# A new order of issue for four engines in a six-layer attention and feed-forward kernel

## The reference

```
for i in range(6):
    x = attn_layer(shift_tokens(x), Wqkv[i], q_scale[i], k_scale[i], Wo[i]) + x
    x = ffn_layer(shift_tokens(x), ln_g[i], ln_b[i], W1[i], b1[i], W2[i], b2[i]) + x
# attn_layer: q, k, v = split(x @ Wqkv); q, k = l2norm(q) * qs, l2norm(k) * ks
#             q, k rotated (cos and sin tables); softmax(8 q k^T, each window of 32 with the one before) @ v; @ Wo
# ffn_layer:  a, gate = split(layernorm(x) @ W1 + b1); a * gelu(gate) @ W2 + b2   (341 inner columns)
```

## Time and profile before

| | |
|---|---|
| median of 3 runs | 3438.64 us (3437.9 to 3438.7) |
| the profiled execution | 3438.64 us, its span 3436.9 us |
| granted TensorE clock, mean | 0.997 |
| PE busy | 3384.2 us (98%) |
| PE weight loads | 2885.9 us (84%) |
| ACT busy | 3077.6 us (90%) |
| DVE busy | 2999.8 us (87%) |
| POOL busy | 2471.8 us (72%) |

### The profile page before, as it was taken

How to read it: one execution, slowest core, us unless ns; L and a number is a source line. 1 busy time by engine, 2 the same in 40 slices (tenths; PEclk the granted TensorE clock), 3 DMA queues, 4 the chain that set the end, 5 groups by cost and what they waited for, 6 DMA issues and landing times. The chain is left out here.

```text
span 3436.9 us, 178950 instructions
## 1 busy us (share of the span) xinstructions
PE 3384.2 (98%) x70388; PEld 2885.9 (84%) x70388; DVE 2999.8 (87%) x7016; ACT 3077.6 (90%) x10549; POOL 2471.8 (72%) x2057
## 2 busy tenths in 40 slices
PE   8999989999999999999999999999999999999998
PEld 5666678888888888888888888888888888888887
DVE  8999989888988888888888988889888888888987
ACT  8999978899999999989999999999999999998886
POOL 0121178787878878788787887878878788787784
PEclk9999999999999999999999999999999999999999
DMA  2000012111221111121111121112211111111111
GB/s 106 8 5 20 5 41 60 49 44 43 54 61 49 46 43 48 55 56 54 41 48 50 55 58 44 49 40 56 59 48 49 41 47 54 50 44 47 53 44 45
DMA packets 177482, 160.67 MB, mean 47 GB/s; under 512 B 113933, under 2 KB 124813, under 8 KB 176397
## 3 DMA queue, kind: packets, MB, share of 16 engines
q1 hardware_dynamic: 176653, 149.22, 15.4%
HBM read 25.71 MB, written 4.19 MB: 9 GB/s over the span
## 5 line engine op out<-in xcount | busy, mean ns | idle before, releaser
L1547 POOL TENSOR_TENSOR a_rn<-a_ssqc,a_minus_half 128x16 f32<-128x16 f32 x384 | 1114.2, 2901 | 477.8 <-DVE a_ssqc L1758 477.2
L1431 ACT ACTIVATE late<-bank,a_negmax 128x64 f32<-128x64 f32 x3072 | 926.6, 326 | 21.3 <-DVE a_negmax L1709 19.4
L1565 POOL TENSOR_TENSOR a_r<-a_u,a_rn 128x512 f32<-128x512 f32 x768 | 806.1, 1050 | 55.8 <-DVE a_u L1740 10.5
L1431 ACT ACTIVATION_READ_ACCUMULATOR late<-bank,a_negmax 128x1 f32 x3072 | 674.9, 220 | 0.0
L1721 DVE TENSOR_TENSOR a_u<-bank,a_rot_c 128x512 f32<-128x512 f32 x768 | 521.3, 679 | 31.9 <-ACT a_sq L1407 31.3
L1733 DVE TENSOR_TENSOR a_v<-bank,a_rot_s 128x512 f32<-128x512 f32 x768 | 522.9, 681 | 0.0
L1740 DVE TENSOR_TENSOR a_u<-a_u,a_v 128x1024 f32<-128x1024 f32 x384 | 469.5, 1223 | 24.2 <-DVE a_v L1733 0.9
L1554 POOL TENSOR_TENSOR a_PN<-late,a_erec 128x256 f32<-128x256 f32 x768 | 473.0, 616 | 12.1 <-PE bank L1079 8.2
L1414 ACT ACTIVATE a_QK<-bank 128x512 f32<-128x512 f32 x768 | 467.8, 609 | 1.7 <-PE bank L1055 1.7
L1055 PE MATMUL bank<-ident,a_r 128*128 128x128 f32 x3072 | 460.8, 273 | 4.2 <-ACT late L1393 2.0
L1751 DVE TENSOR_REDUCE a_ssq<-a_sq 128x16 f32<-128x1024 f32 x384 | 463.7, 1207 | 0.0
(11 more groups left out here) (190 smaller groups left out, 7747.3 us busy)
## 6 DMA issues: line engine op xcount, KB each, us to landing
a_V_sh<-a_V_nat SPq DMA_DIRECT2D x384, 192.0 KB, 2.5
a_V_sh<-a_V_nat SPq DMA_DIRECT2D x192, 64.0 KB, 2.3
late<-in_qkv SPq DMA_DIRECT2D x20, 384.0 KB, 3.6
a_x_sh<-X SPq DMA_DIRECT2D x48, 128.0 KB
a_V_sh<-a_V_nat SPq DMA_DIRECT2D x192, 32.0 KB, 2.1
a_x_sh<-X SPq DMA_DIRECT2D x48, 127.0 KB
late<-X SPq DMA_DIRECT2D x47, 128.0 KB
late<-X SPq DMA_DIRECT2D x47, 127.0 KB
```

The costliest lines, as they stand in the source:

```text
L1431: ins = act.activation(E[:, s.par, k, :], scores[:, hp, col:col + KW], ACT.Exp, bias=negmax[:, s.par, k:k + 1], accum_out=esum[:, s.par, k ...
L1547: pool.tensor_tensor(rn[:, a.par, :], ssqc[:, a.par, :], minus_half[:, :], ALU.pow).then_inc(S["rn"], 1)
L1565: pool.tensor_tensor(heads(r[:, a.par, half]), heads(u[:, a.par, half]), rn[:, a.par, mm * 2 * HG:(mm + 1) * 2 * HG].unsqueeze(2).to_broad ...
```

## The change

The order of the calls inside the four `cycle` functions is changed, and some waits are dropped that other waits imply (`u_rot` before `project`, `exp0` where `exp1` is now the last of the exponentials, `sq` before `sines`). No instruction with data is added, removed or resized. In words:

- PE: in step 3 and 4 an `up` changes place with `project(.., 1)` (up earlier in step 3, later in step 4). In step 6 `up(.., 1, 1, p_tb)` moves behind `values`. In step 7 `transpose_x` moves from ahead of `project(.., 1)` to behind `values`.
- ACT: the four `exps` run in the order (0,0), (0,1), (1,0), (1,1), so that one of them, not two, comes behind `outputs`. `gelu` and the first gate copies come before the second `squares`, `high_x` behind it. Splits of weights go to the end of the step.
- POOL: the two `probs` change places, `deviation` moves from step 2 to the end of step 1.
- DVE: `cosines(a, 0)` and `sines(a, 0)` move ahead of both `reciprocals`, and in step 6 ahead of the second `product`, in step 7 ahead of `low_x`. `feed_forward_out` moves from the end of step 5 to the head of step 6. The weight splits move from the next step to the end of their own.

```diff
@@ -1007,7 +1007,6 @@
                         pe.wait_ge(S["w_lo"], G * a.layer + a.g + 1)
                     ge(pe, S[f"sq{mm}"], a.k)
                     ge(pe, S[f"v_rot{mm}"], a.k)
-                    ge(pe, S["u_rot"], 2 * a.k - 1 + mm)
                     x, m = n % 2, slice((2 * a.half + mm) * P, (2 * a.half + mm + 1) * P)
                     pe.matmul(p_qk[mm][:, :], xh[:, x, m], wh[:, a.g, 0:2 * CQ], start=True, stop=False)
                     pe.matmul(p_qk[mm][:, :], xl[:, x, m], wh[:, a.g, 0:2 * CQ], start=False, stop=False)
@@ -1150,31 +1149,30 @@
                 late_end(n, p)
                 outputs(pair_at(n, p, LAG_O), n * NP + p, done(n, p - 1, LAG_T1))
                 project(n, p, 0)
+                if p == P_GATE:
+                    up(n, p, 0, 0, p_ta)
                 if p == P_X:
                     up(n, p, 2, 1, p_ta)
-                if p == P_X and n + 1 < NI:
-                    transpose_x(n + 1)
+                project(n, p, 1)
+                if p == P_TURN:
+                    turn(n)
+                if p == P_VALUES:
+                    up(n, p, 0, 1, p_ta)
                 if p == P_GATES:
                     up(n, p, 1, 0, p_ta)
-                project(n, p, 1)
-                if p == P_VALUES:
-                    up(n, p, 0, 1, p_ta)
-                if p == P_GATE:
-                    up(n, p, 0, 0, p_ta)
-                if p == P_VALUES:
-                    up(n, p, 1, 1, p_tb)
-                if p == P_TURN:
-                    turn(n)
                 values(n, p)
                 late_pieces(n, p)
                 if p == P_BIAS:
                     shifts(n)
+                if p == P_X and n + 1 < NI:
+                    transpose_x(n + 1)
+                if p == P_VALUES:
+                    up(n, p, 1, 1, p_tb)
                 if p == P_GATES:
                     up(n, p, 2, 0, p_tb)
                 if p == P_GELU:
                     down(n)
                 if s:
-                    ge(pe, S["exp0"], s.k)
                     ge(pe, S["exp1"], s.k)
                 logits(s, p_s)
                 transpose_probs(n, p)
@@ -1203,7 +1201,6 @@
                 if j == -3:
                     for name in ("sq0", "sq1", "v_rot0", "v_rot1"):
                         pe.wait_ge(S[name], NI * NP)
-                    pe.wait_ge(S["u_rot"], 2 * NI * NP)
                 else:
                     pe.wait_ge(S["exp1"], s.k if j == -4 else s.k - 1)
                 logits(s, end_s(s))
@@ -1446,32 +1443,32 @@
                     late_outputs(2 * p - 1)
                 queries_and_keys(pair_at(n, p, LAG_Q1), 1)
                 exps(s, 0, 0, p_s)
+                exps(s, 0, 1, p_s)
+                queries_and_keys(pair_at(n, p, LAG_Q0), 0)
                 exps(s, 1, 0, p_s)
-                queries_and_keys(pair_at(n, p, LAG_Q0), 0)
                 outputs(pair_at(n, p, LAG_O))
                 exps(s, 1, 1, p_s)
-                exps(s, 0, 1, p_s)
                 if p == P_TURN:
                     turned(n)
                 squares(n, p, 0)
+                if p == P_GATES:
+                    gate_out(n, 1, p_ta)
+                if p == P_GELU:
+                    gelu(n)
+                if p == P_GATE:
+                    gate_out(n, 0, p_ta)
+                squares(n, p, 1)
+                if p == P_GATES:
+                    gate_out(n, 2, p_tb)
                 if p == P_X and n + 1 < NI:
                     high_x(n + 1)
+                values(n, p)
+                probs(pair_at(n, p, LAG_PT))
+                if p < 2:
+                    split_up(n, p)
                 split = split_at(n, p)
                 if split:
                     split_qkv(*split)
-                if p == P_GATES:
-                    gate_out(n, 1, p_ta)
-                squares(n, p, 1)
-                if p == P_GELU:
-                    gelu(n)
-                if p < 2:
-                    split_up(n, p)
-                if p == P_GATES:
-                    gate_out(n, 2, p_tb)
-                if p == P_GATE:
-                    gate_out(n, 0, p_ta)
-                values(n, p)
-                probs(pair_at(n, p, LAG_PT))
 
             def end_exps(j, hp):
                 s = end_pair(j)
@@ -1567,13 +1564,13 @@
                                        ALU.mult).then_inc(S[f"r{mm}"], 1)
 
             def cycle(n, p):
+                probs(pair_at(n, p, LAG_S + 1), 0)
+                units(pair_at(n, p, LAG_R + 1), 1)
                 probs(pair_at(n, p, LAG_S + 1), 1)
-                if p == P_NORM + 1 and n >= 2:
-                    deviation(n - 2)
-                units(pair_at(n, p, LAG_R + 1), 1)
-                probs(pair_at(n, p, LAG_S + 1), 0)
                 power(pair_at(n, p, LAG_R))
                 units(pair_at(n, p, LAG_R), 0)
+                if p == P_NORM and n >= 2:
+                    deviation(n - 2)
                 if p == 2 and n >= NI - 4:
                     last_deviation(n - NI + 4)
                 if (n, p) == (1, 0):
@@ -1704,7 +1701,6 @@
             def maxima(s, scores):
                 if s:
                     dve.wait_ge(S["logits"], s.k + 1)
-                    ge(dve, S["exp0"], s.k - 1)
                     ge(dve, S["exp1"], s.k - 1)
                     dve.tensor_reduce(negmax[:, s.par, :].rearrange("p (b i) -> p b i", b=2), scores.rearrange("p b (i k) -> p b i k", i=4), AX.X,
                                       ALU.max, negate=True).then_inc(S["max"], 1)
@@ -1724,10 +1720,7 @@
             def sines(a, mm):
                 if a:
                     m = 2 * a.half + mm
-                    dve.wait_ge(S[f"sq{mm}"], a.k + 1)
                     ge(dve, S["u"], a.k)
-                    if a.first and a.g == 0:
-                        ge(dve, S["rot"], MT * (a.layer - 1) + m + 1)
                     halves = lambda t: t.rearrange("p (s h t f) -> p s h t f", s=2, h=HG, t=2)
                     tab = rot_s[:, m, :, :].rearrange("p s (t f) -> p s t f", t=2).unsqueeze(2).to_broadcast([P, 2, HG, 2, DH // 2])
                     dve.tensor_tensor(halves(v[:, mm * 512:(mm + 1) * 512]), halves(p_qk[mm][:, :])[:, :, :, ::-1, :], tab,
@@ -1787,6 +1780,8 @@
 
             def cycle(n, p):
                 s, a, b = pair_at(n, p, LAG_S), pair_at(n, p, 0), pair_at(n, p, LAG_R)
+                if p == P_GELU + 1:
+                    feed_forward_out(n)
                 maxima(s, p_s)
                 norms(b)
                 cosines(b, 1)
@@ -1794,31 +1789,29 @@
                 sines(b, 1)
                 if p == P_X:
                     residual(n)
-                if p - 1 in (P_TURN, P_GATES, P_GELU):
-                    split_qkv(n, p - 1)
+                if p == P_NORM:
+                    stats(n)
                 if p == P_TURN:
                     norm(n)
-                if p == P_NORM:
-                    stats(n)
                 add(b)
+                if p == P_X:
+                    product(n, 2, p_ta)
                 if p == P_VALUES:
                     product(n, 0, p_ta)
-                reciprocals(s, 0)
+                if p == P_TURN:
+                    turned(n)
+                cosines(a, 0)
+                sines(a, 0)
                 if p == P_BIAS:
                     biases(n)
-                if p == P_TURN:
-                    turned(n)
-                reciprocals(s, 1)
-                if p == P_GELU:
-                    feed_forward_out(n)
+                if p == P_X and n + 1 < NI:
+                    low_x(n + 1)
                 if p == P_VALUES:
                     product(n, 1, p_tb)
-                if p == P_X:
-                    product(n, 2, p_ta)
-                if p == P_X and n + 1 < NI:
-                    low_x(n + 1)
-                cosines(a, 0)
-                sines(a, 0)
+                reciprocals(s, 0)
+                reciprocals(s, 1)
+                if p in (P_TURN, P_GATES, P_GELU):
+                    split_qkv(n, p)
                 if p == P_GATES:
                     split_up(n)
                 if p == 3 and n >= NI - 4:
```

## The result

The changed kernel takes 3486.78 us (median of 4 runs, 3485.86 to 3488.28), the kernel before on the same chip 3438.27 us (4 runs). The ratio is 1.0139, with a 95% interval of 1.0127 to 1.0151: 48.5 us slower, where 32 us were forecast, and 0.8 us above the upper end of the range. The profiled execution has a span of 3483.2 us against 3436.9. Nineteen further executions of the changed kernel, the profiled one among them, have a median of 3485.4 us (3483.7 to 3486.8). So that the time lies above the range at all is within the scatter; that the loss is half as large again as forecast is not.

A forecast was written before the change was run, and what follows sets the result against it. The loop was taken to run at PE's own pace. Terms of 22 + 8.5 - 1.5 + 1.5 + 1.5 = +32 us on 3438.64 us gave 3470 us, 0.9% slower, with a range of 3446 to 3486.

The forecast's parts named there:

- the order of the exponentials: ACT: sum of work ahead of step 6's squares unchanged, exponentials ending about 0.1 us earlier elsewhere; priced at 0.
- Step 6: PE's mm = 1 transposes wait for the later second `product`: 0.48 us in each of 46 iterations, 22 us.
- Step 7: PE's mm = 1 transposes wait for `low_x` after the later `transpose_x`: 0.18 us in 47 iterations, 8.5 us.
- The further wait of step 0: Rival: step 7's wait carries into step 0, DVE's sines hold `project`, 0.3 us per iteration, 14 us, 3485; chance 0.12.
- Layer changes: ACT and DVE weight splits at step ends delay exponentials and maxima: +1.5 us, bounds -3 and +6.
- Last four iterations: Steps 3 and 4: earlier `up` shortens step 3's waits, step 4 waits for DVE again: +1.5 us, bounds -9 and +5.
- Steps 0 to 4 otherwise: Step 3's `up` ahead of `project` covers waits for sines: -1.5 us, bounds 0 and -3; other moves there 0.
- Step 5: `feed_forward_out` moved to step 6's head: no gain on PE's path; DVE's wait ahead of it near 1.5 us.
- The third table load: Rival: ACT's second square behind GELU needs another load each iteration, up to 59 us, about 3530; chance 0.03.

The follow-up runs named there:

- the second-product experiment: Kernel before, with only the second `product` moved behind `cosines` and `sines` on DVE: 3466.15 us, ratio 1.0082.
- the experiment: Changed kernel with `transpose_x`, `high_x` and `low_x` of step 7 put back to their old places: 3475.96 us, ratio 1.0114.
- the split experiment: Changed kernel with ACT's weight splits put back behind the first squares: 3477.67 us, ratio 1.0119.
- the five put back: Changed kernel with step 6, the exponentials' order, step 7, ACT's weight splits and step 4's order put back together: 3442.15 us, ratio 1.0010.

## Why the prediction came out as it did

The direction and the bound were right: PE's own stream sets the pace, the loss is waits put into it, and it came to 1.4% where I had 0.9. The step that failed is the pricing of ACT's new order: I asked whether ACT's sum stays the same and whether the exponentials come late, not who waits for each instruction that comes later. That put the weight splits of the layer changes at 1.5 us, where putting them back gives 7 to 9, and the order of the exponentials at nothing, where it costs 16 us in step 6 when it stands alone. Point by point:

- **Step 6** (forecast 22 us, measured 26.2): the chain squares, `cosines`, `sines`, second product is right to 0.03 us at its end, and the second-product experiment shows it alone at 25.3. PE's mm = 1 transposes start 0.08 us later than forecast: 0.03 by the chain, and 0.05 because PE follows DVE by 0.15 us, not 0.1. The work behind them takes 0.02 us more than before, where 0.03 was forecast. What the prediction missed here is a second chain in the same step: it said that the order of the exponentials leaves ACT's sum the same and costs nothing. The sum is the same, but `outputs` inside it comes later, and `values` and the second `up` wait for it. In the whole change the product would hold PE about as long in any case, so that wait adds only about 1 us; alone it costs 16 us. That the sum for step 6 came near although a chain was missed is luck.
- **Step 7** (8.5, measured 8.9): the chain is as worked out, and the experiment gives it back whole. One figure of it does not follow as written: 0.44 us ahead of 1531.51 is 1531.07, not 1530.98. The trace has `transpose_x` 3.98 us into the step, which is 1530.98. The further wait of step 0 that a rival feared did not come: step 0 changed by 0.5 us over the loop.
- **Layer changes** (1.5, measured 9.1 by the split experiment, 6.6 by the sums over its steps): this is the term of the sum that failed; without its excess the time would lie inside the range. Its upper bound of 6 us was too low as well. I put the splits ahead of the exponentials, which have room, and did not look at what stands first behind them, `queries_and_keys`, nor at who waits for it at the head of PE's next step. DVE's splits cost something too, which no experiment put back: at the end of step 2 they hold the maxima of step 3 in iterations 8, 16, 24, 32 and 40, and with them the exponentials and `queries_and_keys` (in iteration 24 it starts 1.43 us into the step instead of 0.47), for which `up` then waits. That is read from the traces; step 3 is 0.2 to 0.4 us longer in each, 1.5 us in all, and still so with the five put back.
- **Last four iterations** (1.5 with -9 and +5, measured +3.3 in steps 3 and 4): the mechanism is as stated in the main, step 4 gives back what step 3 saves and more. The clock has a part in it: of the 6.5 us that step 3 saves, 4.1 are that its clock fell in two iterations before and in none after.
- **Steps 0 to 4 otherwise**: -1.5 forecast for step 3; it changed by less than 1 us outside the last four and the layer changes. Step 1 costs 1.3 us in the five iterations where splits of the feed-forward weights now stand at the end of steps 0 and 1. About half of that may be the same fault as with the other splits: 0.7 us are left where the five are put back and these splits keep their new place. No run puts these splits back, so this is argued and not shown.
- **Step 5**: `feed_forward_out` off DVE's path gave no gain that can be told, as said; DVE's wait fell to 61.8 / 46 = 1.3 us (forecast 1.5).
- **The third table load** did not come: ACT has 94 loads in either kernel. ACT's timeline in step 5 of the changed kernel:

```profile
1835.95 1.28 ACT L1368 ACT_TABLE_LOAD   x1
1837.25 1.48 ACT L1368 ACTIVATE late<-late 128x1536 f32<-128x1536 f32 x1
1838.64 0.58 ACT L1404 ACTIVATE a_sq<-bank 128x512 f32<-128x512 f32 x1
```

The second squares start right behind GELU. The Trainium skill (ScalarE: Activation LUTs, section on table sets) names four functions that every set has as filler, the square not among them; here it needed no load behind GELU, so the set that serves GELU has it too. Its price was not put to the test.

The terms with their measured sizes: 26.2 in step 6 (1.4 of it from splits), 8.9 in step 7, 3.3 in steps 3 and 4 of the last four iterations, 5.9 for the rest of ACT's splits make 44.3 us, beside 43.4 in the loop; the difference is small gains and losses in steps 0 to 4. From the loop's 43.4 to the 48.5 us between the medians 5.1 us are left. Of these the start of the loop has 2.3, which moves as much from one trace to another, and what comes behind the loop 0.7; the rest, 2.1 us, is that the profiled executions lie 46.4 us apart and the medians 48.5.

The range was drawn too narrow for its own terms. The upper bounds of the prediction add up to 53 us, which is 3492; its end was set at 3486 because they would not all meet.

## What to carry to other kernels

When instructions are only reordered on an engine whose sum stays the same, list for each one that comes later who waits for its count, not only who waits for the last of the group: here it was the copy that frees a shared PSUM bank. Ask of a piece of work moved to the end of a step what stands first in the next one. And where two waits lie in one step, undoing one edit alone shows only part of its price or none: try each from both sides.

## What was not expected of the hardware

In the last four iterations the granted clock fell to 1.2 GHz in some steps in which PE had waited 1.3 to 2.2 us, and not in others with the same wait. In the kernel before, step 3 ran at a mean of 0.72, 1.00, 1.00 and 0.85 in iterations 44 to 47, each time with one wait of 2.22 or 2.23 us. In the changed kernel it ran at 1.00 in all four, with waits of 1.30 to 1.37 us; with step 4 put back, at 0.84 in all four, with waits of 1.27 to 1.38 us. Step 4 of iterations 44 and 46 of the changed kernel ran at 0.85 and 1.00, each with a wait of 1.79 us. A fallen clock added 1.3 to 2.6 us to the step.
